# A 3x3 convolution on TensorE as 32x32 taps in place of 128x64 matmuls, in a Fourier tower of four layers

## The chip, the cores and the metric

One core of a Trainium2 chip. The metric is the device time of one execution in microseconds, the median of three runs. Everything is float32. TensorE is the matmul engine, VectorE, ScalarE and GpSimd (POOL) the others; SyncE (SP) issues most loads. PSUM is where matmuls put their results, in 8 banks of 512 columns.

## The reference

32 images of 64x64 pixels with 3 channels are lifted to 32 channels (`h = concat(grid, x) @ P_w + P_b`). Then four layers run, each of which is a spectral branch and a 3x3 convolution of the same input:

```python
for i in range(nl):
    h_ft = jnp.fft.rfft2(h)
    out_modes = jnp.einsum('bixy,ioxy->boxy', h_ft[:, :, :mx, :my], w_c)      # 16 x 16 modes
    spec = jnp.fft.irfft2(out_modes, s=(H, W))
    conv = lax.conv_general_dilated(h, conv_w[i], (1, 1), 'SAME', dimension_numbers=dn) + conv_b[i]
    h = leaky(spec + conv)
out = leaky(h @ Q1_w + Q1_b) @ Q2_w + Q2_b
```

The result, 32 x 64 x 64, goes through two small attention blocks (the tail, not touched by the change).

## The kernel before, in words

`build_tower` computes the four layers, `build_tail` the rest. The tower works on pairs of images: 16 pairs a layer, so T = 16 l + p runs from 0 to 63. A pixel has a row parity r and a column parity s; the 32 channels of the four parities (r, s) lie on 4 x 32 partitions. What a partition holds of a pair is 64 rows of 32 pixels. Output is made in four units u of 512 pixels each, each in its own PSUM bank (`acc[0]` to `acc[3]`).

On TensorE a pair T needs these groups:
- `convolve(T, u)` (L343 to L366). In layer 0 it is one 96x128 matmul from columns prepared on the host (L355). In layers 1 to 3 it reads `halo` (L365), which is unfolded in one direction: the four partition groups hold the four column phases that two output columns need, and each row parity has its own plane. Three row taps by two output row parities make 6 matmuls of 128x64 with 512 columns. The weights (`conv`) hold zeros where a phase isn't used by a column parity.
- `spectral(T, u)` (L368 to L377): the last step of the inverse transform, added to the same bank: 16 matmuls of 128x32 with 128 columns.
- `rows_forward(n)` (L272), `columns_forward(n)` (L285): forward transforms of the activations of pair n − 2; both are followed by other engines. `columns_back(T)` (L334): the first step of the inverse.
- `mix(l)` (L317): once a layer, the product over channels for all modes, 128 matmuls in four parts.
- in layer 3 `head_hidden` (L380) and `head_out` (L393) in place of the forward transforms.

A float32 matmul appears in the profile as two MATMUL and two LDWEIGHTS records.

The order on every engine is written by hand, and semaphores join them. TensorE's order of a pair is in `pair(l, p, last)` (L400): convolve 0 and 1, spectral 0 and 1, rows_forward, convolve 2 and 3, columns_forward, columns_back of the next pair, spectral 2 and 3. Between layers (L449 to L458) it is rows_forward, convolve 0, columns_forward, convolve 1, mix, convolve 2, columns_back, convolve 3. VectorE transposes (`turn_x` L573 from `x_now` to `xt`; `turn_rows` L580; `turn_modes` L596; `turn_back` L603). ScalarE evicts each unit with bias and leaky ReLU to `x_now` (`evict`, L506), and copies the spectrum (`spectrum`, L489) with 8 activations a pair. GpSimd stores `x_now` to DRAM (L246), and SP loads `halo` for pair T from there (L203), double buffered, when pair T − 2 has left it. `rows_forward`, `columns_back` and their transposes share the banks 4 and 5 (`turned`), `columns_forward` uses bank 6. `convolve(T, u)` waits only for the eviction of the same unit of the pair before (L346).

## Time and profile before

| | us |
|---|---|
| median of 3 runs (range) | 1410.2 (1409.04 to 1412.42) |
| the profiled execution | 1409.31 |
| its span, first to last instruction | 1407.5 |
| TensorE busy in the span | 1268.3 (90%) |
| VectorE busy | 546.8 (39%) |
| ScalarE busy | 492.0 (35%) |
| mean granted TensorE clock | 0.945 of 2.4 GHz |
| MATMUL records, LDWEIGHTS records | 17040, 17040 |

A MATMUL record lasts until its result is written, so records overlap, and busy time counts a stretch that holds at least one. In the timeline a row merges the records of one group: its start, the time from the first start to the last end, engine, line, operation, the operands with the shape of one record, the count, and in brackets the idle time before it and what ended that. The time for which a group holds the array is read from the start of the next one.

### The profile page before, as it was taken

What the parts mean: (1) busy time and instruction counts of PE and PEld (TensorE: products, weight loads), DVE (VectorE), ACT (ScalarE), POOL (GpSimd) and SP (SyncE); (2) the same over time, 40 slices, a digit from 0 to 9 for tenths busy, and PEclk for the clock granted to TensorE, in tenths of its full rate; (3) what the DMA queues carried; (4) which work ended last, traced back from release to release, by engine and by line L of the source; (5) the groups of instructions that cost most, each with busy time, mean ns of one, the idle gap of its engine ahead of it and who ended that gap; (6) DMA issues with size and microseconds to landing.
All of it is one profiled execution on the core that took longest, in us unless ns stands there. A gap on an engine that the chain in (4) does not pass through costs nothing. (4 is left out here: it accounts for less than half of the span.)

```text
span 1407.5 us, 36967 instructions
## 1 busy us (share of the span) xinstructions
PE 1268.3 (90%) x17040; PEld 694.0 (49%) x17040; DVE 546.8 (39%) x553; ACT 492.0 (35%) x934; POOL 66.7 (5%) x122
## 2 busy tenths in 40 slices
PE   4888889899999998999999989999999962889955
PEld 2555455544444444444444445444444422579945
DVE  3655555333335332433343332111111103567775
ACT  1244344233333332233333322443444431425511
POOL 2000000000000000000000000111111010000000
PEclk7899999999999999999999999999999976879967
DMA  8434344776666666766666664555555507000000
GB/s 273 156 119 117 112 128 126 248 205 186 186 186 188 189 191 178 239 189 189 188 193 197 180 193 103 123 119 117 116 115 117 115 4 153 2 1 1 2 0 15
DMA packets 39338, 192.19 MB, mean 137 GB/s; under 512 B 16432, under 2 KB 16560, under 8 KB 17456
## 3 DMA queue, kind: packets, MB, share of 16 engines
q1 hardware_dynamic: 30224, 137.39, 38.3%
q0 software_dynamic: 8960, 52.44, 10.3%
q8 instruction: 134, 2.20, 0.7%
q14 instruction: 20, 0.16, 0.0%
HBM read 136.84 MB, written 52.95 MB: 135 GB/s over the span
## 5 line engine op out<-in xcount | busy, mean ns | idle before, releaser
L365 PE MATMUL psum<-halo,conv 128*64 128x512 f32 x2304 | 521.1, 600 | 0.0
L365 PEld LDWEIGHTS psum<-halo,conv 128*64 128x64 f32 x2304 | 156.4, 137 | 326.7 <-issue 288.4
L603 DVE STREAM_TRANSPOSE vt<-psum 128x1024 f32<-128x1024 f32 x64 | 127.4, 1990 | 391.0 <-PE psum L341 391.0
L489 ACT ACTIVATE spec<-psum 32x128 f32<-32x128 f32 x384 | 150.5, 392 | 299.2 <-PE psum L294 295.3
L506 ACT ACTIVATE x_now<-psum,conv_bias 128x512 f32<-128x512 f32 x256 | 169.8, 687 | 243.7 <-PE psum L376 226.2
L376 PEld LDWEIGHTS psum<-dft,vt 128*32 128x32 f32 x8192 | 216.0, 110 | 76.9 <-issue 72.4
L376 PE MATMUL psum<-dft,vt 128*32 128x128 f32 x8192 | 250.2, 274 | 1.0 <-DVE vt L603 1.0
L573 DVE STREAM_TRANSPOSE xt<-x_now 128x1024 f32<-128x1024 f32 x100 | 124.1, 1243 | 283.3 <-PE psum L282 186.3
L580 DVE STREAM_TRANSPOSE ft<-psum 128x1024 f32<-128x1024 f32 x50 | 95.1, 1901 | 12.6 <-PE psum L282 12.6
L294 PEld LDWEIGHTS psum<-dft,ft 128*64 128x64 f32 x1600 | 55.1, 141 | 62.3 <-DVE ft L580 43.0
L294 PE MATMUL psum<-dft,ft 128*64 128x64 f32 x1600 | 57.5, 227 | 27.1 <-DVE ft L580 27.1
L341 PE MATMUL psum<-zt,dft 64*64 64x256 f32 x1024 | 71.8, 393 | 0.3 <-DVE zt L596 0.3
L513 ACT ACTIVATE xt<-psum,q1b 128x512 f32<-128x512 f32 x64 | 40.5, 684 | 87.8 <-PE psum L389 87.8
L521 ACT ACTIVATE ft<-psum,q2b 4x512 f32<-4x512 f32 x64 | 43.5, 680 | 77.1 <-PE psum L397 76.5
L282 PE MATMUL psum<-xt,dft 64*32 64x512 f32 x800 | 57.9, 638 | 12.9 <-DVE xt L573 12.9
L355 PE MATMUL psum<-xcol,conv 96*128 96x512 f32 x128 | 65.5, 634 | 0.0
L246 POOL DMA_DIRECT2D activations<-x_now x48 | 25.7, 535 | 804.5 <-ACT x_now L506 804.5
L773 PE MATMUL t_psum<-t_consts 128*128 128x128 f32 x212 | 28.2, 299 | 26.3 <-DMA t_consts<-in_tail 26.3
L341 PEld LDWEIGHTS psum<-zt,dft 64*64 64x64 f32 x1024 | 35.7, 133 | 25.8 <-issue 15.6
L253 POOL DMA_DIRECT2D tower_out<-ft x64 | 31.6, 501 | 287.6 <-ACT ft L521 287.5
L773 PEld LDWEIGHTS t_psum<-t_consts 128*128 128x128 f32 x212 | 27.6, 215 | 29.7 <-DMA t_consts<-in_tail 28.1
L950 ACT ACTIVATE t_prob<-t_dif 128x512 f32<-128x512 f32 x32 | 20.2, 631 | 59.6 <-DVE t_dif L1065 59.6
(133 smaller groups left out, 785.4 us busy)
## 6 DMA issues: line engine op xcount, KB each, us to landing
activations<-x_now POOLq DMA_DIRECT2D x48, 1056.0 KB, 10.1
halo<-activations SPq DMA_DIRECT2D x192, 264.0 KB, 6.5
halo<-activations SPq DMA_DIRECT2D x192, 263.9 KB, 6.2
wspec<-in_spec SPq DMA_DIRECT2D x16, 1024.0 KB, 9.5
xcol<-in_xcol SPq DMA_DIRECT2D x16, 384.0 KB, 4.4
x_now<-in_ser SPq DMA_DIRECT2D x2, 1056.0 KB, 6.6
t_lq<-in_onehot SPq DMA_DIRECT2D x1, 2048.0 KB, 15.3
t_kr<-in_causal SPq DMA_DIRECT2D x1, 2048.0 KB, 23.9
```

The costliest lines, as they stand in the source:

```text
L282: z = mm(turned[g:g + 32, r, :], ex[64 * r:64 * r + 64, :], xt[64 * r:64 * r + 64, 32 * h + m:32 * h + 32:2, :], start=True, stop=True)
L294: z = mm(ap_[64 * h:64 * h + 64, 64 * kyb:64 * kyb + 64], ft[:, k0:k0 + 2, :].rearrange("p a c -> p (a c)"), ey[:, ri, :], start=(ri == 0) ...
L341: z = mm(turned[64 * il:64 * il + 64, cg, 256 * ri:256 * ri + 256], iy[64 * cg:64 * cg + 64, m, :], zt[64 * cg:64 * cg + 64, :, 2 * p:2 * ...
L355: mm(acc[u], conv0[:], xcol[:, k, HALF * u:HALF * u + HALF], start=True, stop=False, skip_group_check=True)
L365: mm(acc[u][64 * r:64 * r + 64, :], conv[:, l - 1, dy, :], rows[:, at:at + 16, 0:G], start=(dy == 0), stop=False, skip_group_check=True)
L376: z = mm(acc[u][g:g + 32, 128 * ih:128 * ih + 128], vt[:, k, 4 * u + ih, r, :], ix[:, s, :], start=False, stop=True, skip_group_check=True)
L489: z = copy(spec[g:g + 32, 64 * qh:64 * qh + 64, ql, 2 * p:2 * p + 2] .rearrange("p (y x) b -> p y b x", x=MODES), ap_[32 * q:32 * q + 32]. ...
L506: copy(x_now[:, k, 16 * u:16 * u + 16, 0:G], acc[u].rearrange("p (i j) -> p i j", j=G), ACT.Prelu, bias=conv_bias[:, l:l + 1], alpha=SLOPE ...
L573: vec.transpose(xt[:, 32 * h:32 * h + 32, :], x_now[:, n % 2, 32 * h:32 * h + 32, 0:G]).then_inc(s_xt, 1)
L580: vec.transpose(ft[:].rearrange("p k c -> p c k"), turned.rearrange("p a b -> p (a b)").rearrange("p (i c) -> p c i", c=C)).then_inc(s_ft, 1)
L603: vec.transpose(vt[:, k].rearrange("p h r o -> p (h r) o").rearrange("p y o -> p o y"), turned.rearrange("p a b -> p (a b)").rearrange("p ...
L773: mm(bank(b)[:, 0:128], ident, ident, start=True, stop=True)
```

## The change

The convolution of layers 1 to 3 is written as nine taps of 32 channels by 32 channels. `halo` now holds every pixel once: the four parities f on 4 x 32 partitions, one plane, with zero rows around. For a tap, input parity f feeds output parity f ^ d, where d says which of row and column parity differ: d = 3 has 4 taps (both differ), d = 1 and d = 2 have 2, d = 0 has 1. For each tap, 16 matmuls of 32x32 with 512 columns are issued, one for each input parity f and output position `to`; the unit is u = f ^ d ^ to. So that the four units of one tap fall on different positions, the output parities of unit u are permuted by u (`turn`), and the other matmuls and the halo's loads of layers 2 and 3 (16 DMAs of 16 rows in place of 8) undo it. All four units are started together, and the convolution of a pair is cut into four segments, `taps(T, 3)`, `(T, 1)`, `(T, 2)`, `(T, 0)`; each waits for the last matmul of the segment before (`s_seg`). `rows_forward`, `columns_forward` and `columns_back` are cut into twice as many, smaller matmuls. The banks are shared otherwise: `rowed` (4, 5), `backed` (6, 7), `columned` (4). The orders of TensorE, ScalarE and VectorE are changed. `head_out` writes all 128 partitions, and `head_read` is one activation. In the cut diff below the removed lines of the old `convolve`, `pair` and the order between layers are left out (they stand above), as are the layout of weights on the host and the constants.

```diff
-PAD = 2 * PITCH
-HALO = 2 * PLANE + PAD
+UNIT = 16 * PITCH
+TOP = 1 + 2 * PITCH
+HALO = TOP + PLANE + 2 * PITCH + 1
...
-        turned = psum[:, 4:6, :]
-        ap_ = psum[:, 6, 0:256]
+        rowed = psum[:, 4:6, :]
+        backed = psum[:, 6:8, :]
+        hidden = psum[:, 4:6, :]
+        valued = psum[:, 4, :]
         spare = psum[:, 7, :]
+
+        def columned(n):
+
+            return psum[:, 6 if n < 2 else 4, 0:256]
...
+        def turn(l, u):
+
+            return u if l > 0 else 0
...
+                if src >= 2:
+                    sp.wait_ge(s_acc, 4 * (T - 2) + 4)
+                if l == 1:
+                    sp.dma_start(halo[:, k, TOP:TOP + PLANE], x_d[p]).then_inc(s_halo[k], 16)
+                    return
+                for u in range(4):
+                    for f in range(4):
+                        g = 32 * (f ^ turn(l - 1, u))
+                        sp.dma_start(halo[32 * f:32 * f + 32, k, TOP + UNIT * u:TOP + UNIT * u + UNIT],
+                                     x_d[p, g:g + 32, UNIT * u:UNIT * u + UNIT]).then_inc(s_halo[k], 16)
...
+                if n > 2:
+                    pe.wait_ge(s_spec, n)
+                l = (n - 2) // PAIRS if n >= 2 else 0
+                for i in range(2):
+                    for m in range(2):
+                        for h in range(2):
+                            for f in range(2):
+                                u, g = 2 * h + i, 64 * m + 32 * h
+                                at = 16 * u + m
+                                z = mm(rowed[g:g + 32, f ^ (turn(l, u) // 2), 256 * i:256 * i + 256],
+                                       ex[64 * f:64 * f + 64, turn(l, u) % 2, :],
+                                       xt[64 * f:64 * f + 64, at:at + 15:2, :], start=True, stop=True)
                 z.then_inc(s_fx, 1)
...
-                            k0 = ri * MODES + 4 * kyb + 2 * h
-                            z = mm(ap_[64 * h:64 * h + 64, 64 * kyb:64 * kyb + 64],
-                                   ft[:, k0:k0 + 2, :].rearrange("p a c -> p (a c)"), ey[:, ri, :],
-                                   start=(ri == 0), stop=(ri == 1))
+                            for i in range(2):
+                                k0, g = ri * MODES + 4 * kyb + 2 * h + i, 64 * h + 32 * i
+                                z = mm(columned(n)[g:g + 32, 64 * kyb:64 * kyb + 64], ft[:, k0, :], ey[:, ri, :],
+                                       start=(ri == 0), stop=(ri == 1))
                 z.then_inc(s_fy, 1)
...
+                reached(pe, s_vt, T)
                 for m in range(4):
                     il, ri = m // 2, m % 2
-                    for cg in range(2):
-                        z = mm(turned[64 * il:64 * il + 64, cg, 256 * ri:256 * ri + 256],
-                               iy[64 * cg:64 * cg + 64, m, :],
-                               zt[64 * cg:64 * cg + 64, :, 2 * p:2 * p + 2, :].rearrange("p k b o -> p k (b o)"),
-                               start=True, stop=True)
+                    for h in range(2):
+                        for cg in range(2):
+                            g = 64 * il + 32 * h
+                            z = mm(backed[g:g + 32, cg, 256 * ri:256 * ri + 256],
+                                   iy[64 * cg:64 * cg + 64, m, 32 * h:32 * h + 32],
+                                   zt[64 * cg:64 * cg + 64, :, 2 * p:2 * p + 2, :].rearrange("p k b o -> p k (b o)"),
+                                   start=True, stop=True)
                 z.then_inc(s_v, 1)
...
+            def convolve_first(T):
+
+                k, p = T % 2, T % PAIRS
+                pe.wait_ge(s_xcol[k], 16 * (p // 2 + 2))
+                for u in range(4):
+                    reached(pe, s_x, 4 * (T - 1) + u + 1)
+                    mm(acc[u], conv0[:], xcol[:, k, HALF * u:HALF * u + HALF], start=True, stop=False,
+                       skip_group_check=True)
+
...
+            def taps(T, d):
 
                 l, p = place(T)
                 k = T % 2
+                if d == 3:
+                    pe.wait_ge(s_x, 4 * T)
+                    pe.wait_ge(s_halo[k], halo_loads(T))
+                else:
+                    pe.wait_ge(s_seg, 3 * (T - PAIRS) + {1: 1, 2: 2, 0: 3}[d])
+                for dy in ((-1, 1) if d & 2 else (0,)):
+                    for dx in ((-1, 1) if d & 1 else (0,)):
+                        w = 3 * (dy + 1) + dx + 1
+                        for f in range(4):
+                            r, s = (f ^ d) // 2, (f ^ d) % 2
+                            di, dj = (r + dy - f // 2) // 2, (s + dx - f % 2) // 2
+                            for to in range(4):
+                                u = f ^ d ^ to
+                                at = TOP + (16 * u + 2 * di) * PITCH + dj
+                                rows = halo[32 * f:32 * f + 32, k, at:at + UNIT].rearrange("p (i j) -> p i j", j=PITCH)
+                                z = mm(acc[u][32 * to:32 * to + 32, :], conv[32 * f:32 * f + 32, l - 1, w, :],
+                                       rows[:, :, 0:G], start=(d == 3 and dy == -1 and dx == -1), stop=False,
+                                       skip_group_check=True)
+                if d > 0:
+                    z.then_inc(s_seg, 1)
+                elif p > 0:
+                    z.then_inc(s_acc, 2)
 
...
-                            g = 64 * r + 32 * s
+                            g = 32 * ((2 * r + s) ^ turn(l, u))
                             z = mm(acc[u][g:g + 32, 128 * ih:128 * ih + 128], vt[:, k, 4 * u + ih, r, :],
                                    ix[:, s, :], start=False, stop=True, skip_group_check=True)
-                z.then_inc(s_acc, 1)
+                if u >= 2 or l == 0 or p == 0:
+                    z.then_inc(s_acc, 1)
...
+            def first_pair(p):
+                T = p
+                if p > 0:
+                    convolve_first(T)
+                    rows_forward(T + 1)
+                    if p < LAST:
+                        columns_back(T + 1)
+                for u in range(4):
+                    spectral(T, u)
+                if p > 0:
+                    columns_forward(T + 1)
+                else:
+                    columns_back(T + 1)
+            def pair(l, p):
 
                 T = l * PAIRS + p
+                if p == 0:
+                    for u in range(4):
+                        spectral(T, u)
+                    columns_back(T + 1)
+                    return
+                taps(T, 3)
+                rows_forward(T + 1)
+                if p < LAST:
+                    columns_back(T + 1)
+                taps(T, 1)
+                spectral(T, 0)
+                taps(T, 2)
+                spectral(T, 1)
+                taps(T, 0)
+                spectral(T, 2)
+                spectral(T, 3)
+                columns_forward(T + 1)
+            def last_pair(p):
+                T = (NL - 1) * PAIRS + p
+                if p == 0:
+                    for u in range(4):
+                        spectral(T, u)
+                    columns_back(T + 1)
+                    return
+                taps(T, 3)
+                head_hidden(p - 1, 0)
+                taps(T, 1)
+                head_hidden(p - 1, 2)
+                taps(T, 2)
+                head_out(p - 1)
                 spectral(T, 0)
                 spectral(T, 1)
+                taps(T, 0)
+                spectral(T, 2)
+                spectral(T, 3)
                 if p < LAST:
                     columns_back(T + 1)
+            def boundary(l):
+                T = l * PAIRS
+                taps(T, 3)
+                rows_forward(T + 1)
+                taps(T, 1)
+                columns_forward(T + 1)
+                pe.wait_ge(s_spec, T + 2)
+                mix(l)
+                columns_back(T)
+                taps(T, 2)
+                taps(T, 0)
 
...
-                copy(hid[:, u, :], psum[:, 6 + u % 2, :], ACT.Prelu, bias=q1b[:], alpha=SLOPE).then_inc(s_hid, 1)
+                copy(hid[:, u, :], hidden[:, u % 2, :], ACT.Prelu, bias=q1b[:], alpha=SLOPE).then_inc(s_hid, 1)
...
-                for u in range(4):
-                    z = copy(h_now[32 * u:32 * u + 4, k, :], psum[32 * u:32 * u + 4, 6, :], ACT.Identity,
-                             bias=q2b[32 * u:32 * u + 4, :])
-                z.then_inc(s_h, 1)
+                copy(h_now[:, k, :], valued, ACT.Identity, bias=q2b[:]).then_inc(s_h, 1)
 
...
                 if last and p > 0:
-                    head_activate(p - 1, 0)
-                    head_activate(p - 1, 1)
-                evict(T, 0)
-                evict(T, 1)
-                if p > 0:
-                    if last:
-                        head_activate(p - 1, 2)
-                        head_activate(p - 1, 3)
-                        head_read(p - 1)
-                    else:
-                        spectrum(T - 1)
-                evict(T, 2)
-                evict(T, 3)
+                    for u in range(4):
+                        head_activate(p - 1, u)
+                    head_read(p - 1)
+                for u in range(4):
+                    evict(T, u)
+                if p > 0 and not last:
+                    spectrum(T - 1)
                 if p == LAST and not last:
                     spectrum(T)
             for u in range(4):
...
-                    if not last:
-                        turn_x(T + 2, 0)
-                        if p > 0:
-                            turn_rows(T + 1)
+                    if p > 0 and not last:
+                        turn_rows(T + 1)
                     if p < LAST:
                         turn_back(T + 1)
                     if not last:
+                        turn_x(T + 2, 0)
```

The three calls `convolve(0, 0..3)` around `project` and `mix(0)` become one `convolve_first(0)` after `columns_back(0)`. The order of layer 0 is `first_pair`, that of layers 1 and 2 `pair`, of layer 3 `last_pair`, and `boundary(l)` runs ahead of each layer but the first.

## Rows read from the trace of the kernel before

**Rows 1.** Stretches, layer 1: us; busy of PE, PEld, DVE, ACT, POOL; clock; DMA share, GB/s.
```profile
282.00:542.00 260.00, 260.00 (x3612) 126.73 (x3604) 99.55 (x64) 85.54 (x177) 7.97 (x15) 1.00 0.66 191
```

**Rows 2.** Timeline of TensorE, layer 1, one pair and the starts around it.
```profile
600.29 1.09 PE L282 MATMUL psum<-xt,dft 64*32 64x512 f32 x16
601.31 5.37 PE L365 MATMUL psum<-halo,conv 128*64 128x512 f32 x24
606.51 1.10 PE L294 MATMUL psum<-dft,ft 128*64 128x64 f32 x32
607.54 1.11 PE L341 MATMUL psum<-zt,dft 64*64 64x256 f32 x16
608.58 1.96 PE L376 MATMUL psum<-dft,vt 128*32 128x128 f32 x64
610.46 5.37 PE L365 MATMUL psum<-halo,conv 128*64 128x512 f32 x24
615.76 1.95 PE L376 MATMUL psum<-dft,vt 128*32 128x128 f32 x64
617.65 1.09 PE L282 MATMUL psum<-xt,dft 64*32 64x512 f32 x16
```

**Rows 3.** Timeline of TensorE, layer 0, one pair.
```profile
218.65 1.09 PE L282 MATMUL psum<-xt,dft 64*32 64x512 f32 x16
...
222.99 1.15 PE L294 MATMUL psum<-dft,ft 128*64 128x64 f32 x32 [1.34 <-DVE ft L580]
...
230.79 1.09 PE L282 MATMUL psum<-xt,dft 64*32 64x512 f32 x16
```

**Rows 4.** Timeline of TensorE, layer 3, one pair.
```profile
1056.83 1.09 PE L389 MATMUL psum<-x_now,q1w 32*32 32x512 f32 x16
1057.85 1.96 PE L376 MATMUL psum<-dft,vt 128*32 128x128 f32 x64
...
1075.25 1.09 PE L389 MATMUL psum<-x_now,q1w 32*32 32x512 f32 x16
```

**Rows 5.** Line L797 in the tail: durations min/median/max, starts, form.
```profile
L797 PE MATMUL t_psum<-t_zT,t_uT x64: 218/218/267, 1190.1 to 1191.1; 64*64 64x64 f32 x64
```

**Rows 6.** Timeline of ScalarE in the pair of rows 2.
```profile
600.42 0.69 ACT L506 ACTIVATE x_now<-psum,conv_bias 128x512 f32<-128x512 f32 x1 [0.18 <-PE psum L376]
607.66 3.24 ACT L489 ACTIVATE spec<-psum 32x128 f32<-32x128 f32 x8 [6.54 <-PE psum L294]
610.92 1.27 ACT L506 ACTIVATE x_now<-psum,conv_bias 128x512 f32<-128x512 f32 x2
```

**Rows 7.** Line L203, the halo's loads: issue, landing; and the queue of instructions.
```profile
L203 SPq DMA_DIRECT2D halo<-activations x384: 302/422/2221, 239.3 to 1110.8; - x192
...
DMA to landing us min/median/max: 3.0/6.5/11.5
...
q8 instruction: 134, 2.20, 0.7%
```

**Rows 8.** Timeline of TensorE and VectorE between layers 0 and 1.
```profile
248.36 1.95 PE L376 MATMUL psum<-dft,vt 128*32 128x128 f32 x64
...
255.29 4.45 PE L365 MATMUL psum<-halo,conv 128*64 128x512 f32 x12
...
263.90 7.69 PE L329 MATMUL psum<-spec,wspec 128*64 128x64 f32 x256 [0.66 <-ACT spec L489]
...
277.86 1.95 PE L376 MATMUL psum<-dft,vt 128*32 128x128 f32 x64
...
271.63 1.25 DVE L596 STREAM_TRANSPOSE zt<-psum 128x1024 f32<-128x1024 f32 x1 [0.62 <-PE psum L329]
```

**Rows 9.** Timeline after mix(0), and ScalarE at the tower's end.
```profile
54.96 1.12 PE L355 MATMUL psum<-xcol,conv 96*128 96x512 f32 x2
...
59.54 1.96 PE L376 MATMUL psum<-dft,vt 128*32 128x128 f32 x64 [1.00 <-DVE vt L603]
...
1140.83 2.75 ACT L521 ACTIVATE ft<-psum,q2b 4x512 f32<-4x512 f32 x4 [4.97 <-PE psum L397]
```

More of the change, by code:

```diff
@@ L1300, in tower_inputs @@
     spec[:, :, 1, ..., 0, :], spec[:, :, 1, ..., 1, :] = wi, wr
+    values = np.zeros((4, C, 2, C), np.float32)
+    for g in range(4):
+        for e in range(2):
+            values[g, :, e, g ^ (2 * e)] = np.asarray(t["L0_tok_Q2_w"])[:, 0]
     four = lambda b: np.tile(np.asarray(b).reshape(-1), 4).reshape(128, 1)
```

139 lines of the change are left out of this document (35 added, 104 removed).

## The prediction

> **What bounds the kernel now.** I first read the table of stretches: in layer 1 TensorE is busy for all of a stretch of 260 us, at the full granted clock (1.00, the 2.4 GHz level), while VectorE and ScalarE are busy 38% and 33% of it [rows 1]. So only TensorE's list of groups matters there, and I read its timeline by starts, since the next group's start is where the array was given over. One image pair of layers 1 and 2 takes 617.65 − 600.29 = 17.36 us [rows 2]: convolve of two units 5.20, columns_forward 1.03, columns_back 1.04, spectral of two units 1.88, convolve 5.30, spectral 1.89, rows_forward 1.01. Layer 0 takes 12.14 us a pair, of it 1.34 us of waiting for VectorE's transpose before columns_forward [rows 3]. Layer 3 takes 18.42 [rows 4].
>
> **What a group costs.** A float32 matmul shows as two records. In convolve a record has 512 columns and two run side by side (64 output columns each): 24 records in 5.16 us plus a change of group is 0.43 us per record and tile. The same 0.43 explains rows_forward (16 records on 8 tiles of 64x32: 0.86, measured 1.02) and head_hidden (16 records on 8 tiles of 32x32: 0.86, measured 1.02) [rows 2, 4]. So the price is rounds x 0.43 us plus about 0.15 us for a change of tile shape. Over one pair: 10.32 (convolve) + 3 x 0.86 (rows, columns, back) + 3.49 (spectral: 128 records on 4 tiles at 0.109 us a round) = 16.39; the other 0.97 us is six changes of shape, 0.16 each.
>
> **The convolution.** 24 matmuls of 128x64 become 144 of 32x32 a pair (segments 3, 1, 2, 0 have 64, 32, 32, 16), so 48 records become 288. Before, a quarter of the weights fed were zeros (each output parity uses three of the four column phases); now only the nonzero taps run. If 16 tiles run side by side the price is 288/16 = 18 rounds x 0.43 = 7.74 us against 10.32. The trace shows no 16 tiles at once. The bound below is that, 7.74. The bound above is the most tiles that it does show, 8 [rows 4]: 288/8 x 0.43 = 15.5 us. Which is nearer? What could cap it is start spacing, weight loads or outputs. Start spacing: on 64x64 tiles with 64 columns, 64 records start within 1.0 us (1190.1 to 1191.1), 16 ns a record [rows 5], and the taps need 27 ns (7.74 us / 288), the pace at which spectral already runs (1.88 us for 64 [rows 2]). Loads: spectral also loads 32 columns for each record at that pace. Different data to four column tiles of one row group is what spectral does. What is unproved is four row groups times four column groups, and four banks written for each 32 partitions; two are shown (rows_forward). I take 16 tiles.
>
> One rule speaks against the change. In each round one bank takes output of four row groups, at four different quarters of the partitions. In head_hidden four row groups write one bank at different quarters too, and two units of it take 1.02 us, the 8-tile price [rows 4]. The Trainium skill, page TensorEngine Tiling (Array Packing), section Gotcha 1: PSUM Pressure, says that different row tiles cannot access the same bank at the same time. By that rule head_hidden would have taken 8 rounds of 2, 3.4 us; the trace does not agree, and I price nothing for it. For 16 tiles only a page has a price: the Trainium skill, page TensorE: Matmul & The Clock Gate, section Measured speedup vs the span model, gives one duration plus 4 ns for each further tile; the taps would then cost what I take, and no row here shows it.
>
> **The new pair, layers 1 and 2**, in order of the code: four tap segments 7.74, plus for each a change of shape and a start staggered over 16 tiles, 0.21 (estimate, from 0.16 with 8 tiles): 8.58. rows_forward 1.02. columns_back is now 32 records on 8 tiles of the same shape as rows_forward: 0.96. spectral 0 and spectral 1 alone: 0.87 + 0.14 = 1.01 each. spectral 2 and 3: 1.88. columns_forward, now 64 records of 64 columns on 4 tiles: at 16 ns a record [rows 5], no change of shape: 1.0. Sum 15.46, a gain of 1.90. 15 pairs in each of two layers: **57 us**.
>
> **Its waits.** taps(T, 3) starts all four units, so it waits for the eviction of unit 3 of the pair before; behind it all of TensorE is queued. An eviction starts 0.13 us after the group behind its spectral starts and takes 0.69 us [rows 6], two back to back 1.27. Units 0 and 1 are released after taps(T, 0), so from the start of spectral 2: evictions start at 0.2, 0.8, 1.4 and 2.0 and the last ends at 2.7, while columns_forward ends at 1.88 + 1.0 = 2.9. Hidden, with 0.2 us to spare. rows_forward now waits for ScalarE's spectrum (it shares bank 4 with it): 3.24 us from 0.12 us after columns_forward [rows 6], ending at 3.4, against 3.65 for the first tap segment. Hidden, 0.25 to spare. If either cover fails by 0.3 us, 45 pairs cost 13 us: for the range. The wait of taps on its own last segment is covered by the group between, except once a layer (0.16 us).
> Halo loads: half the bytes, 1 DMA a pair in layer 1 and 16 in layers 2 and 3 in place of 8. SP needs 16 x 0.42 = 6.8 us to issue them and the landing is 6.5 [rows 7]: 13.3 us after the release, and 16.4 are there (columns_forward and one pair). Priced at nothing; with the longest landing, 11.5, 2 us late. Queued behind them on SP is only the next pair's load, on POOL nothing changes.
>
> **Layer 0.** convolve_first of four units together 3.63, rows_forward 1.02, columns_back 0.96, spectral 3.63, columns_forward 1.03: 10.3 against 12.14, since VectorE's 1.9 us transpose now lies behind columns_back and spectral. 15 pairs x 1.84 = **28 us**.
>
> **Layer 3.** taps, head_hidden, taps, head_hidden, taps are all of one tile shape: 3.44 + 0.86 + 1.72 + 0.86 + 1.72 + 0.6 of starts = 9.2; head_out 0.98, spectral 1.88, taps 1.07, spectral 1.88, columns_back 1.04: 16.05 against 18.42. ScalarE's two activations of hid (1.27) lie behind 1.8 us of taps. 15 x 2.37 = **35 us**.
>
> **Boundaries, start and end.** From the last spectral of a layer (248.36 + 1.88) to the first of the next (277.86) it is 27.6 us [rows 8]; there are three such boundaries. The 3.95 us wait for xt goes: the first tap segment lies in front of it. What is late next: mix now waits 3.4 us for spectrum with nothing in front of it, and columns_back 1.5 us for the last transpose of mix (1.25 us, from 0.21 after mix). Sum: 3.65 + 1.02 + 1.93 + 0.22 + 1.03 + 3.4 + 7.5 + 1.5 + 1.03 + 1.93 + 0.16 + 1.07 = 24.5. At 255.29 the first 12 records of convolve took 4.28 in place of 2.7 us after such an idle stretch, so the 3.4 us may cost up to 1.7 in mix: gain 1.4 to 3.1 a boundary, I take the middle, **7 us** for three. Start: 54.96 to 59.54 is 4.58 us, and it becomes 1.4 + 1.03 + 3.63 = 6.1, as all of convolve_first lies behind columns_back: **−1.5** [rows 9]. End: head_read is one activation of 0.69 in place of four, 2.75 us, twice on the path (before the evictions at 1143.6 and at the very end): **+4** [rows 9].
>
> **Sum.** 57 + 28 + 35 + 7 − 1.5 + 4 = 129.5 us. The profiled execution took 1409.3 us (span 1407.5), 0.9 below the median shown, 1410.2. 1410.2 − 129.5 = 1280.7, and I say 1280.
>
> **Rivals.**
> *Hand-offs or instructions bind, not the array.* A pair has 2 x 544 PE instructions in place of 2 x 240. The queue of instructions moved 2.20 MB in 134 pieces [rows 7], 64 bytes for each of the 34080 matmul and load instructions; the fastest long stretch of the trace, mix, takes 512 of them in 7.5 us (7.69 with the end of the last) [rows 8]. If that were the most that can be fed, a pair would take 1088/512 x 7.5 = 15.9 us, 0.5 more: with the thin covers above failing too, 0.5 to 1 us in 45 pairs, 1300 to 1325. Against it: 16 ns a record in [rows 5], though for 1 us only.
> *The array holds only 8 of these tiles at once.* Place: every tap segment. Then 15.5 us of taps, a pair of 23.2 us: 45 x 7.74 = 348 more than forecast, 1628. It decides from below about 13 tiles at once, where 288 x 0.43 / n exceeds the 9.6 us at which a pair is even. For it: nothing in the trace is wider than 8. Against it: nothing in the starts of head_hidden, 8 tiles within one 0.43 us round, looks like a limit.
>
> **How the numbers follow.** Forecast and its close variants (1262 to 1295) 0.72; fed or handed over late (1295 to 1340) 0.16; tiles capped, slower 0.10; the rest 0.02. The low end, 1262, is 0.1 us less for each start of a tap segment (45 x 4 x 0.1 = 18 us); the high end, 1330, takes in most of the second case. A measurement of this kernel tells 0.2% (3 us) from no change; forecast and second case are faster, the third slower.
>
> **What would show it.** In the profile after: a tap record every 27 ns, 18 rounds of 0.43 in a pair; starts of rows_forward 15.5 us apart in layers 1 and 2, 10.3 in layer 0, 16.0 in layer 3; no idle of TensorE before taps (ScalarE's eviction) or before rows_forward (spectrum); a 3.4 us idle before mix. Wrong if the taps' busy time over 45 pairs is far from 8.6 us a pair, or if idle time of TensorE put down to ScalarE or to issue passes 10 us in the tower.

## The result: slower, 1429.7 us against 1409.7

The changed kernel took 1429.71 us, median of 4 runs (1425.49 to 1434.98), against 1409.65 for the kernel before in the same session (4 runs, 1409.04 to 1412.42): ratio 1.014, 95% interval 1.0096 to 1.0185. The prediction was 1280 (1262 to 1330). Of all executions reported here one, 1412.62 us of e1_wide, is over 1.5% above the fastest of its kernel at a lower granted clock (0.931), and its ratio leaves it out. The profiled execution took 1425.49 us, span 1423.7, the fastest of the four; the 16.2 us over the profiled execution of before is what has to be explained, and the 145.7 us by which the forecast (1409.3 − 129.5 = 1279.8) fell short of it.

### Where the time went, by layer

From here a layer's span is the time from the last `spectral` record of its pair 0 to that of its pair 15, and a boundary the time from there to the last one of the next layer's pair 0, both read from the trace:

| us | layer 0 | layer 1 | layer 2 | layer 3 | three boundaries |
|---|---|---|---|---|---|
| before | 185.9 | 259.3 | 259.3 | 275.1 | 98.4 |
| after | 162.1 | 300.5 | 274.3 | 258.7 | 103.4 |
| pair before | 12.14 | 17.36 | 17.36 | 18.42 | |
| pair after | 10.25 to 11.9 | 17.7 to 24.1 | 16.9 to 20.9 | 17.25 | |

Sum: −23.8 + 41.2 + 15.0 − 16.4 + 5.0 = +21.0; outside the tower's pairs 4.8 came back. So two layers gained, two lost, and in the two that lost the pairs differ by 4 and 6 us. Before, nearly all pairs of a layer were alike. The written order is the same for each of them, which points to something from outside it.

The page of after: busy by engine, queues (packets, MB, share), and the costliest groups.

```profile
PE 1258.6 (88%) x31984; PEld 798.9 (56%) x31984; DVE 546.4 (38%) x553; ACT 453.6 (32%) x886; POOL 67.0 (5%) x121
...
q8 instruction: 251, 4.11, 1.2%
...
L399 PE MATMUL psum<-halo,conv 32*32 32x512 f32 x13824 | 536.1, 603 | 12.9 <-issue 12.7
...
L399 PEld LDWEIGHTS psum<-halo,conv 32*32 32x32 f32 x13824 | 217.1, 103 | 201.8 <-issue 140.3
```

TensorE is busy 9.7 us less than before, yet the kernel is slower: idle time has come in, and its releaser is "issue", no engine and no data. The queue of instructions moves 251 pieces in place of 134 [rows 7]. Layer 1, the stretch of [rows 1], is now:

```profile
282.00:542.00 260.00, 236.85 (x6983) 127.11 (x6967) 84.70 (x55) 71.09 (x154) 6.46 (x13) 0.96 0.34 111
```

TensorE was busy for all 260.00 us of it before, and is for 236.85. The clock column has fallen too, from 1.00 to 0.96. In the trace's record of the clock this is 20.5 us in layer 1 at the 1.2 GHz level, in four stretches (from 291.9, 387.4, 466.0 and 506.9 us). The first follows 0.9 us after an idle of TensorE of 1.04 us, the others begin within idles of 1.45, 2.39 and 3.56 us. In layer 1 of before there is no such stretch, and none in layers 2 and 3 of either kernel. The timeline of TensorE in after, in order of time: a pair of layer 0 [rows 3], the first boundary [rows 8], a gap in layer 1, one undisturbed pair of layer 2 [rows 2], a pair of layer 3 [rows 4].

```profile
80.23 1.09 PE L302 MATMUL psum<-xt,dft 64*32 64x256 f32 x32
...
90.48 0.88 PE L302 MATMUL psum<-xt,dft 64*32 64x256 f32 x24
...
239.56 9.23 PE L350 MATMUL psum<-spec,wspec 128*64 128x64 f32 x256 [3.20 <-ACT spec L563]
250.15 1.13 PE L365 MATMUL psum<-zt,dft 64*32 64x256 f32 x32 [1.35 <-DVE zt L661]
...
257.33 2.38 PE L416 MATMUL psum<-dft,vt 128*32 128x128 f32 x76 [0.91 <-issue]
...
308.40 1.08 PE L399 MATMUL psum<-halo,conv 32*32 32x512 f32 x14
310.85 2.23 PE L399 MATMUL psum<-halo,conv 32*32 32x512 f32 x50 [1.37 <-issue]
...
622.44 1.09 PE L302 MATMUL psum<-xt,dft 64*32 64x256 f32 x32
623.32 1.27 PE L365 MATMUL psum<-zt,dft 64*32 64x256 f32 x32
624.53 2.35 PE L399 MATMUL psum<-halo,conv 32*32 32x512 f32 x64
626.81 1.08 PE L416 MATMUL psum<-dft,vt 128*32 128x128 f32 x32
627.82 2.35 PE L399 MATMUL psum<-halo,conv 32*32 32x512 f32 x64
630.10 1.08 PE L416 MATMUL psum<-dft,vt 128*32 128x128 f32 x32
631.11 1.16 PE L399 MATMUL psum<-halo,conv 32*32 32x512 f32 x32
632.19 1.96 PE L416 MATMUL psum<-dft,vt 128*32 128x128 f32 x64
633.97 1.08 PE L316 MATMUL psum<-dft,ft 128*32 128x64 f32 x64
634.97 4.46 PE L399 MATMUL psum<-halo,conv 32*32 32x512 f32 x128
639.37 0.88 PE L302 MATMUL psum<-xt,dft 64*32 64x256 f32 x24
...
1054.14 1.07 PE L439 MATMUL psum<-xt,q2w 128*32 128x512 f32 x8
...
1071.38 1.07 PE L439 MATMUL psum<-xt,q2w 128*32 128x512 f32 x8
```

The undisturbed pair, by starts: 639.37 − 622.44 = 16.93 us, where 15.46 was forecast. The four tap segments hold the array for 4.40, 2.28, 2.28 and 1.08 us: 10.04, where 8.58 was forecast; all else together takes 6.89, and 6.88 was forecast. And most pairs of layer 1 aren't undisturbed: between 308.40 and 310.85 TensorE has put 14 of the segment's 64 records out and waits for nothing that the profile shows.

### Two theories

**A, the feed.** A pair is 1088 PE instructions in 17 us. Instructions come in pieces of 16 KB, 256 instructions, one per 4 us at this rate. In the trace's list of packets pieces start at 298.34, 301.65, then only at 308.41, and again at 311.99. Between 301.65 and 308.41 the pair's halo load (issued at 301.10) and the store of the pair before it (issued at 302.04) hold the same DMA engines:

```profile
301.10 0.32 SPq L215 DMA_DIRECT2D halo<-activations  x1
302.04 0.53 POOL L261 DMA_DIRECT2D activations<-x_now  x1 [19.98 <-ACT x_now L580]
```

Each landed 6 to 8 us after it was issued, and the gap of TensorE follows. It ends at 310.85, 2.43 us after the start of the late piece. The same holds through the whole layer: from 262.5 to 560 us TensorE has 16 gaps over 0.2 us, and each of them ends 2.2 to 2.6 us after the start of a piece that itself came 5.5 to 8.6 us after the one before it, where the median is 4.0. Layer 3 has halo loads but no store, 57 PE instructions per us in place of 64, and no gap. The waits of TensorE around layer 1, from 260 to 560 us (total, times, longest; short ones aren't listed):

```profile
PE psum L399 <- issue: 12.2, 9, 3.6
PE psum L302 <- issue: 8.1, 4, 2.8
PE psum L365 <- issue: 5.9, 3, 2.4
```

**B, the array.** Even undisturbed, the taps take 17% more than was forecast for 16 tiles at 0.43 us a round. The starts of matmuls in the segment at 607.02 (first records, from the trace): 16 from 607.022 to 607.122, one each 7 ns; the 17th at 607.905, as soon as the first tile is free; but the 18th only at 608.098, and then one each 16.7 ns. The first matmul's second record ended at 607.475 + 0.587 = 608.06 (starts are measured, the ends of TensorE's records are modelled). It stays so in the four-tap segment at 634.97: the 18th starts 0.036 us after the end of the first, and each of the 39th to the 48th 0.035 to 0.037 us after the end of the one 17 before it. So either TensorE holds no more than 17 float32 matmuls (68 instructions: two loads, two passes each) that haven't completed (window, W), or 16 tiles at once stream more slowly for a reason in the array or its output (R).

A rival to both: **C**, DMA traffic slows matmuls themselves, not their feed.

### The profile page after: what moved, and what is told of

Same layout as the page of the kernel before. It is cut to its first block and busy times, and to the rows that moved or that the text cites. A ratio compares the mean times of both kernels' runs of the same rounds, so it can differ in the third digit from the quotient of the medians.

```text
span 1423.7 us, 67011 instructions
## 1 busy us (share of the span) xinstructions
PE 1258.6 (88%) x31984; PEld 798.9 (56%) x31984; DVE 546.4 (38%) x553; ACT 453.6 (32%) x886; POOL 67.0 (5%) x121
## 5 line engine op out<-in xcount | busy, mean ns | idle before, releaser
L399 PE MATMUL psum<-halo,conv 32*32 32x512 f32 x13824 | 536.1, 603 | 12.9 <-issue 12.7
L399 PEld LDWEIGHTS psum<-halo,conv 32*32 32x32 f32 x13824 | 217.1, 103 | 201.8 <-issue 140.3
L416 PEld LDWEIGHTS psum<-dft,vt 128*32 128x32 f32 x8192 | 218.6, 110 | 113.6 <-issue 105.0
L416 PE MATMUL psum<-dft,vt 128*32 128x128 f32 x8192 | 256.2, 275 | 3.6 <-issue 3.5
L365 PE MATMUL psum<-zt,dft 64*32 64x256 f32 x2048 | 85.8, 384 | 17.2 <-issue 11.8
L302 PE MATMUL psum<-xt,dft 64*32 64x256 f32 x1600 | 62.1, 397 | 15.5 <-issue 14.3
L365 PEld LDWEIGHTS psum<-zt,dft 64*32 64x32 f32 x2048 | 47.2, 107 | 37.3 <-issue 18.0
L316 PE MATMUL psum<-dft,ft 128*32 128x64 f32 x3200 | 56.9, 221 | 8.3 <-issue 4.2
L302 PEld LDWEIGHTS psum<-xt,dft 64*32 64x32 f32 x1600 | 26.0, 109 | 66.8 <-issue 58.8
L316 PEld LDWEIGHTS psum<-dft,ft 128*32 128x32 f32 x3200 | 52.4, 111 | 13.7 <-DVE ft L645 7.4
L431 PE MATMUL psum<-x_now,q1w 32*32 32x512 f32 x512 | 54.8, 593 | 2.2 <-ACT xt L587 1.4
L350 PE MATMUL psum<-spec,wspec 128*64 128x64 f32 x1024 | 35.3, 239 | 11.6 <-ACT spec L563 9.6
```

The source lines that it names most:

```text
L302: z = mm(rowed[g:g + 32, f ^ (turn(l, u) // 2), 256 * i:256 * i + 256], ex[64 * f:64 * f + 64, turn(l, u) % 2, :], xt[64 * f:64 * f + 64, ...
L316: z = mm(columned(n)[g:g + 32, 64 * kyb:64 * kyb + 64], ft[:, k0, :], ey[:, ri, :], start=(ri == 0), stop=(ri == 1))
L365: z = mm(backed[g:g + 32, cg, 256 * ri:256 * ri + 256], iy[64 * cg:64 * cg + 64, m, 32 * h:32 * h + 32], zt[64 * cg:64 * cg + 64, :, 2 * p ...
L399: z = mm(acc[u][32 * to:32 * to + 32, :], conv[32 * f:32 * f + 32, l - 1, w, :], rows[:, :, 0:G], start=(d == 3 and dy == -1 and dx == -1) ...
L416: z = mm(acc[u][g:g + 32, 128 * ih:128 * ih + 128], vt[:, k, 4 * u + ih, r, :], ix[:, s, :], start=False, stop=True, skip_group_check=True)
L431: z = mm(hidden[to:to + 32, u % 2, :], q1w[32 * g:32 * g + 32, :], x_now[32 * g:32 * g + 32, p % 2, 16 * u:16 * u + 16, 0:G], start=True, ...
```

## The experiments

Ratios with an interval come from 4 or more runs of each kernel; the others are one execution.

### e1_wide: fewer instructions, the same taps

```diff
-                            for i in range(2):
-                                k0, g = ri * MODES + 4 * kyb + 2 * h + i, 64 * h + 32 * i
-                                z = mm(columned(n)[g:g + 32, 64 * kyb:64 * kyb + 64], ft[:, k0, :], ey[:, ri, :],
+                            k0 = ri * MODES + 4 * kyb + 2 * h
+                            z = mm(columned(n)[64 * h:64 * h + 64, 64 * kyb:64 * kyb + 64],
+                                   ft[:, k0:k0 + 2, :].rearrange("p a c -> p (a c)"), ey[:, ri, :],
...
```

(and `columns_back` in its old 64-wide form.)

> The changed kernel with columns_forward and columns_back as wide as before (16 and 8 matmuls a pair in place of 32 and 16), so 992 in place of 1088 TensorE instructions a pair; nothing else differs. Theory A (in layers 1 and 2 TensorE starves for instructions, whose 16 KB pieces queue behind the burst of halo load and store at the end of each pair): fewer instructions to feed, so the mean pair falls from 20.0 us (layer 1) and 18.3 us (layer 2) by 0.3 to 1 us, 10 to 30 us in all, 1400 to 1420. Rival B (the idle time is a wait for the halo or the spectrum, shown as issue): no gain, perhaps 0.1 us a pair lost by two more changes of tile shape, 1430 to 1440.

Measured 1388.8 us (1383.35 to 1412.62), ratio 0.983 [0.978, 0.988]: 41 us less than after, beyond the 10 to 30 expected. A clean pair takes 17.09 us, 0.16 longer than in after; the spans of layers 1 and 2 fell to 286.6 and 257.2, that of layer 3 stayed (258.5). Instructions that cost the array nothing cost the kernel time where data moves. That is A, with a steeper price than I gave it.

### e2_twelve: three of four output positions

```diff
-                            for to in range(4):
+                            for to in range(4 if d == 3 and w == 0 else 3):
```

(The outputs of position 3 lack eight of their nine taps, so the convolution is incomplete.)

> The changed kernel in which the taps leave out the output position 3 (12 of 16 tiles, 108 + 4 of 144 matmuls a pair), except in the first tap of segment 3. Theory W (TensorE holds about 64 instructions, that is 16 float32 matmuls, until they complete, so a matmul of a tile starts only when the one 16 before it is complete: 1.07 us a tap in place of 0.86): with 12 tiles the window reaches a third of a tap ahead, the two taps of segment 1 take 1.9 to 2.0 us in place of 2.28, and segment 3 about 3.8 in place of 4.40. Rival R (16 streams contend for SBUF or PSUM, cost in proportion to the tiles): each tap still takes over 1.0 us, 2.1 to 2.2 for two, and starts within a tap are not spaced at 7 ns.

```profile
587.92 2.21 PE L399 MATMUL psum<-halo,conv 32*32 32x512 f32 x48
590.07 1.08 PE L416 MATMUL psum<-dft,vt 128*32 128x128 f32 x32
```

Two taps took 2.15 us (2.28 with 16 tiles), one execution 1352.7. By size alone this is R's 2.1 to 2.2, and W's 1.9 to 2.0 missed. The starts decide, and against R, which had said that they are not 7 ns apart: 12 from 587.924, one each 7 ns; then 13 to 17 from 588.809, one each 7 ns as their tiles come free; and the 18th at 589.000, though its tile was free. The first matmul's second record ended at 588.376 + 0.588 = 588.964. With 12 tiles as with 16 it is the 18th that waits, for completion of the first. My 1.9 to 2.0 for W had left out that the first five are taken at the tile's pace and the rest at 16.7 ns.

### e9_eight: eight tiles at a time

```diff
-                            for to in range(4):
+                                for to in (2 * half, 2 * half + 1):
```

(with `for half in range(2)` around the taps of a segment.)

> The changed kernel in which each tap segment runs its taps first on the output positions 0 and 1 and then on 2 and 3, so that 8 of 16 tiles are at work at a time; the same 144 matmuls a pair. Theory W (a matmul waits for the completion of the one 17 before it): with 8 tiles the 17th matmul is two rounds later, 1.75 us, and the first is complete by then, so the window never bites: every round takes 0.43 us, segments of two taps 3.6 to 3.7 us, four taps 7.1, one tap 1.9, together 16.3 us a pair of convolution, a pair 23.2, and at 47 instructions a us there are no gaps: about 1620 to 1640. Rival (a stall of 0.2 us at every 17th matmul, whatever is in flight): 0.4 us more in a segment of two taps, 0.8 in one of four, the pair 25.

```profile
631.55 3.08 PE L400 MATMUL psum<-halo,conv 32*32 32x512 f32 x64
634.55 1.08 PE L417 MATMUL psum<-dft,vt 128*32 128x128 f32 x32
```

1518.4 us; a clean pair 20.43 us, where W had 23.2 and 1620 to 1640 in all: both missed. Two taps take 3.00 us: not the 3.44 of 8 rounds, because the second half, on tiles that are idle, starts inside the first half's last rounds. Here the tiles of the second half had been idle from the start, yet only its first matmul begins early (at 0.64 us, as no. 17 of the program), and no. 18 at 1.08, just after the first of all completes (0.454 + 0.587 = 1.04). Why no. 17 doesn't start sooner stays open. So the 16 tiles do run side by side in after: its taps take 10.04 us a pair, and some 13.5 here. The rival of "8 tiles at once" is out, since what 8 at a time costs is measured, and after does not show it. The third part of W's expectation, no gaps, missed too: layer 1 took 317.5 us, 11 more than 15 clean pairs, with idle time put down to issue.

### e10_onepass: two instructions a matmul in place of four

```diff
-                                z = mm(acc[u][32 * to:32 * to + 32, :], conv[32 * f:32 * f + 32, l - 1, w, :],
-                                       rows[:, :, 0:G], start=(d == 3 and dy == -1 and dx == -1), stop=False,
+                                z = mm(acc[u][32 * to:32 * to + 32, :],
+                                       conv[32 * f:32 * f + 32, l - 1, w, :].bitcast(BF16)[:, 1::2],
+                                       rows[:, :, 0:G].bitcast(BF16)[:, :, 1::2], start=(d == 3 and dy == -1 and dx == -1), stop=False,
```

> The changed kernel in which the taps read only the upper two bytes of each number in the halo and in the weights, as bf16: the convolution is less exact, and a matmul is one load and one pass in place of two of each. It asks what the window counts. If it holds 64 to 68 instructions, 32 to 34 such matmuls, two whole taps, are in flight: 0.213 us a tap, the four taps of segment 3 in 1.0 to 1.1 us. If it holds 17 matmuls of any kind, a tap takes about 0.41 us and segment 3 1.4 to 1.5 us. Either way few gaps, since 288 instructions a pair are gone.

```profile
608.97 0.69 PE L400 MATMUL psum<-halo,conv 32*32 32x512 bf16 x32
609.59 1.08 PE L418 MATMUL psum<-dft,vt 128*32 128x128 f32 x32
...
617.80 1.10 PE L303 MATMUL psum<-xt,dft 64*32 64x256 f32 x32 [1.16 <-ACT spec L565]
...
622.01 0.68 PE L400 MATMUL psum<-halo,conv 32*32 32x512 bf16 x29 [1.72 <-issue]
```

Two taps, 32 matmuls, take 0.62 us, with no stall before the 18th: the second 16 start 0.25 us after the first, while the first matmul still runs (its record lasts 0.41 us). Were the limit 17 matmuls of any kind, or the outputs of 16 tiles, it would be here too. Here 17 matmuls are 34 instructions and not 68. That fits a limit on instructions; one on weight loads or on passes alone, of which a float32 matmul has two each, would look the same. So B is W, and what exactly its window counts is shown only so far. The run, 1201.35 us, also shows what is next: its pairs in layer 1 take 13.1 to 18.3 us, in layer 3 12.06, with idle time put down to issue and, for the first time, to ScalarE's spectrum.

### e3_paced: the halo load in four parts

```diff
...
                 for u in range(4):
+                    reached(sp, s_seg, 3 * (T - 1 - PAIRS) + min(u + 1, 3) if T > PAIRS else 0)
+                    if l == 1:
+                        sp.dma_start(halo[:, k, TOP + UNIT * u:TOP + UNIT * u + UNIT],
+                                     x_d[p, :, UNIT * u:UNIT * u + UNIT]).then_inc(s_halo[k], 16)
+                        continue
...
```

(The old load for l = 1 and the new count that TensorE waits for aren't shown.)

> The changed kernel with the halo load of pair T cut into four units, each issued only after a tap segment of pair T - 1, so that loads no longer run together with the store and no megabyte of loads stands ahead of an instruction piece. Theory A: the gaps of 1.5 to 2.3 us once a pair in layer 1 go or halve, layer 1 falls from 20.0 to 17.5 to 18.5 us a pair, layer 2 from 18.3 to 17.3 to 18, together 30 to 55 us: 1375 to 1400. Rival C (the rate of instructions alone is too high for the feed, 64 a us, whatever the data do): within 10 us of 1430.

1427.1 us (1419.86 to 1436.39), ratio 1.0138 [1.0076, 1.02]: no gain, a miss. Layer 1 did what A says (271.5 in place of 300.5), but in layer 2 the load is now itself late, since its last 8 DMAs are issued only after the third segment:

```profile
590.30 2.73 PE L401 MATMUL psum<-halo,conv 32*32 32x512 f32 x33 [2.96 <-DMA halo<-activations]
```

Layer 2 took 296.6: from 560 to 870 us TensorE waits 28.2 us for the halo, and 4.3 us of idle time are put down to issue, 12.7 in after. A burst was traded for a wait on data.

### e4_quiet: the same instructions, no traffic

```diff
+                if T >= PAIRS + 2:
+                    return
                 sp.wait_ge(s_store[src % 2], 16 * (src // 2 + 1))
...
-            for X in range((NL - 1) * PAIRS):
+            for X in range(PAIRS):
```

(The kernel leaves out the loads that bring the pixels of later pairs, so its convolution reads old ones.)

> The changed kernel with halo loads only for the first two pairs of layer 1 and no stores after layer 0; the later pairs convolve what lies in the halo, so almost no data move by DMA in layers 1 to 3. Every TensorE instruction stays. Theory A: no gaps, 16.9 to 17.1 us for each pair of layers 1 and 2 (17.0 is what the fastest pairs of the changed kernel take), about 1425 - 75 = 1350. Rival C (instruction rate alone): pairs stay at 18 to 20 us, over 1400.

```profile
607.15 1.09 PE L303 MATMUL psum<-xt,dft 64*32 64x256 f32 x32
...
624.08 1.09 PE L303 MATMUL psum<-xt,dft 64*32 64x256 f32 x32
```

1356.05 us. Pairs take 16.93 us nearly everywhere, spans 256.4 and 258.2 in layers 1 and 2; layer 0, whose traffic is kept, is as in after. All 251 pieces are fetched. The granted clock of layers 1 and 2 is 1.00. So traffic is what makes the gaps. It tells A from "1088 instructions a pair are too many by themselves", but not from C. For that I read two tap segments of after by stretches, a two-tap one and the four-tap one at 634.97 (the last two columns are the DMA engines' share and GB/s):

```profile
624.53:626.81 2.28, 2.28 (x68) 0.81 (x65) 2.28 (x2) 0.00 (x0) 0.00 (x0) 1.00 0.65 150
...
634.97:639.37 4.40, 4.40 (x136) 2.13 (x129) 1.22 (x2) 3.11 (x8) 0.53 (x1) 1.00 0.84 308
```

In the midst of 308 GB/s the four taps last 4.40 us, as here (619.69 to 624.08) with next to none. Traffic does not slow matmuls that TensorE has; C is out. The run also shows what the change is worth with hardly a gap: 1409.3 − 1356.1 = 53 us, not 130.

### e5_storelate: the store after the load, not beside it

```diff
                 pool.wait_ge(s_x, 4 * X + 4)
+                if X >= PAIRS:
+                    pool.wait_ge(s_seg, 3 * (X + 1 - PAIRS) + 2)
```

> The changed kernel with the store of pair X, in layers 1 and 2, issued only after the second tap segment of the next pair, some 8 us later, so that it no longer runs right behind the halo load. Theory A (an instruction piece waits behind load and store together): the gap after each pair shortens from about 2 us to below 1, layer 1 from 20.0 to about 18.5 us a pair, layer 2 from 18.3 to 17.5: 1385 to 1410. Rival D (each burst of a megabyte by itself is enough to delay a piece, so two bursts at two places cost as much as one long one): 1420 to 1440.

1382.28 us (1381.13 to 1388.43), ratio 0.982 [0.980, 0.984]; layer 1 at 269.8, layer 2 at 265.6, a little better than the 1385 to 1410 expected. No part of these layers ran at the lower clock. The same bytes and the same instructions, 47 us less than after. This is the cleanest run for A: only when a transfer starts was changed.

### e6_order: the kernel before with the new order alone

```diff
+            def first_pair(p):
+
+                T = p
+                if p > 0:
+                    for u in range(4):
+                        convolve(T, u)
+                    rows_forward(T + 1)
+                    if p < LAST:
+                        columns_back(T + 1)
+                for u in range(4):
+                    spectral(T, u)
```

(with the banks `rowed`, `backed`, `columned`, and ScalarE's and VectorE's order in layer 0; the convolution is the old one.)

> The kernel before, with its convolution of 128x64 matmuls and its halo, and of the change only the order and the banks: first_pair for layer 0, evictions ahead of the spectrum there and at a layer's last pair, separate banks for rows_forward, columns_back and columns_forward, and convolve ahead of rows_forward between layers. By the sum of the prediction for these parts: layer 0 12.14 to 10.4 us a pair (26 us), the three boundaries 3 to 4 us each, the start 1.5 lost: 1410 - 34 = 1376, 1370 to 1385. Rival: if the gain of layer 0 came from the smaller matmuls and not from the order, layer 0 stays at about 12 us a pair and the kernel at 1400 or above.

1377.44 us (1375.77 to 1378.51), ratio 0.978 [0.976, 0.979]. Layer 0 took 155.8 (pairs 10.4), layers 1 to 3 were as before (17.36, 18.42). The last two boundaries fell from 33.7 and 32.3 to 29.6 and 30.1; the first rose from 32.4 to 36.2, with TensorE waiting 4.21 us for the halo before its convolution. So 32 us of what the change offered had nothing to do with taps, and the rest of the change, the taps with the smaller matmuls and the order around them, lost 1429.7 − 1377.4 = 52 us on top.

### e7_shapes: the taps in three shapes, 80 matmuls in place of 144

```diff
...
+                if d == 4:
+                    for o in range(4):
+                        for u in range(4):
+                            z = one(u, o ^ u, 0, 128, 9 + o, 0, 0)
+                elif d == 2:
+                    for s in range(2):
+                        for r in range(2):
+                            for u in range(4):
+                                o = 2 * r + s
+                                z = one(u, o ^ u, 64 * (1 - r), 64, 13 + s, -1 if r == 0 else 1, 0)
...
```

(Taps that read the same pixel offset from all four parities are one matmul of 128 rows, those from two parities one of 64 rows, the other three of 32; with e1's `columns_forward`.)

> The changed kernel with the nine taps in three tile shapes: four taps that read the same offset as one 128x32 matmul, two as one 64x32, three as 32x32: 80 matmuls a pair in place of 144, the same 9 rounds of the array; columns_forward as wide as before. Theory W (16 to 17 float32 matmuls at most are in flight): the 128x32 and 64x32 rounds run at 0.86 us, only the three 32x32 rounds at 1.07: convolution 8.4 us in place of 10.05, a clean pair 15.4 to 15.7 us in place of 16.93. Theory A: 768 in place of 1088 instructions a pair, so few gaps: 1409 - 26 (layer 0) - 50 (layers 1, 2) - 35 (layer 3) = 1290 to 1320. Rival R (contention of many streams): the 64x32 segment too takes over 2.1 us and the pair stays above 16.3.

```profile
599.95 3.64 PE L393 MATMUL psum<-halo,conv 128*32 128x512 f32 x32
603.52 1.09 PE L302 MATMUL psum<-xt,dft 64*32 64x256 f32 x32
604.41 1.24 PE L365 MATMUL psum<-zt,dft 64*32 64x256 f32 x30
...
607.33 1.08 PE L435 MATMUL psum<-dft,vt 128*32 128x128 f32 x32
608.34 2.35 PE L393 MATMUL psum<-halo,conv 32*32 32x512 f32 x64
610.62 1.08 PE L435 MATMUL psum<-dft,vt 128*32 128x128 f32 x32
611.63 1.16 PE L393 MATMUL psum<-halo,conv 32*32 32x512 f32 x32
...
619.26 1.09 PE L302 MATMUL psum<-xt,dft 64*32 64x256 f32 x32
```

**1292.18 us (1289.79 to 1292.73), ratio 0.917 [0.915, 0.918]: the fastest of all kernels with the whole float32 convolution.** Only nonzero weights run, as in after, but four tiles of 128 rows at a time fill the array with 4 matmuls. The four-tap segment takes 3.57 us (4.40 in after): 8 rounds of 0.43 and a start. The two-tap segment of 64x32 tiles takes 2.05 us (605.28 to 607.33) and starts while columns_back's last records run, that of 32x32 tiles 2.28. A pair takes 15.74 us, under the 16.3 that R asked for and 0.04 above W's range; the convolution takes 9.0 us, where W had 8.4. And with 768 PE instructions a pair the feed keeps up; of TensorE's long waits in layer 1 put down to issue this is left:

```profile
PE psum L393 <- issue: 0.2, 1, 0.2
```

### e8_shapes_late: both cures together

```diff
                 pool.wait_ge(s_x, 4 * X + 4)
+                if X >= PAIRS:
+                    pool.wait_ge(s_seg, 3 * (X + 1 - PAIRS) + 2)
```

(on e7_shapes.)

> e7_shapes with the store of layers 1 and 2 issued after the second tap segment of the next pair. If the store right behind the halo load still costs gaps in e7_shapes, this is 5 to 20 us faster than it; if there are none left, within 3 us of it.

1296.22 us (1296.11 to 1305.51), ratio 0.922 [0.919, 0.925]: no better than e7, rather 4 us worse, for which no run gives a cause; layers 1 and 2 take 239.7 and 235.9 us, in e7 238.8 and 235.9. Where the feed keeps up, moving the store buys nothing. What was worth 47 us on one kernel is worth nothing on the other, and that is what A asks for.

## Why the prediction was wrong

**The step that failed first** is "If 16 tiles run side by side the price is 288/16 = 18 rounds x 0.43 = 7.74 us". They do run side by side, but a new matmul also waits until the one 17 places ahead has completed, and for most of them that is later than their tile being free (1.08 us after its start, by the 18th, against 0.88, by the 17th). A tap costs 1.1 us, not 0.86. Over a pair 10.04 against 8.58 (with starts): 1.47 us, in 30 pairs 44 us. With the 1.2 us by which layer 3's 17.25 exceeds the forecast 16.05 (15 pairs, 18 us) this is 62 of the 146 us missed. I had bounded the price by the number of tiles, 8 or 16, and had "start spacing, weight loads or outputs" as what could cap it. How many matmuls may be unfinished was not on the list, since in before no group has more than 8 tiles at work.

**The second** is the price of the rival "Hand-offs or instructions bind": "0.5 more", "0.5 to 1 us in 45 pairs". The rival was right that instructions can come too late, and wrong in how. It set a highest mean rate, and there is no such limit in reach here: the undisturbed pairs are fed 1088 instructions in 16.93 us, and e4 feeds nearly all pairs so. What the runs show is single pieces that come late behind a burst of data, up to 8.6 us after the one before where 4.0 is the median. I had taken the rate from mix, in a stretch where the DMA engines were idle. The prediction's own sign of this, over 10 us of idle time put down to issue, came out at 42 us on four lines of the page alone (L302, L399, L365, L416). Against pairs of 16.93 us it cost 300.5 − 254 = 46.5 us in layer 1, 274.3 − 254 = 20.3 in layer 2, none in layer 3; in layer 0, against the forecast's 10.3, 7.6. Together 74 of the 146. Not all of it is waiting: in the 20.5 us of layer 1 at 1.2 GHz TensorE worked for 19, and at full clock would have needed half of that, so about 9.5 of the 46.5 us (an estimate) are the clock that fell after gaps. The prediction had priced a fallen clock only at the boundaries.

**Boundaries** were to give 7 us and cost 5.0: 12 more. The two idles came as forecast, 3.20 before mix (3.4) and 1.35 before columns_back (1.5), and mix ran after the first at a granted clock that averaged 0.67 of the full one for 3.5 us, so 9.23 us in place of 7.69 [rows 8]. I had priced that at up to 1.7. What was not in the sum are again the gaps of the feed, 0.91 and more. The start and end gained 4.8 where 2.5 was forecast. Sum: 44 + 18 + 74 + 12 − 2 = 146.

**What held.** Eviction and spectrum are covered: inside the pairs of layers 1 and 2 TensorE waits for neither. ScalarE in the pair of the timeline:

```profile
614.93 2.48 ACT L580 ACTIVATE x_now<-psum,conv_bias 128x512 f32<-128x512 f32 x4 [18.36 <-PE psum L399]
617.61 3.19 ACT L563 ACTIVATE spec<-psum 32x128 f32<-32x128 f32 x8 [0.21 <-PE psum L316]
```

The evictions end at 617.41, 0.05 us before the next pair's taps start at 617.46 (I had said 0.2 to spare); the spectrum ends at 620.80, 1.6 before rows_forward. The halo was never late, layer 0's clean pair is 10.25 as forecast, and different row groups writing one bank cost nothing that the starts show: 16 tiles in four banks start 7 ns apart.

**The rivals.** "8 tiles at once" would give 1518 (e9), not 1628. The slower side of my forecast held 0.10 and named the wrong mechanism; what made the kernel slower than before was the window and the late instructions, each of them less than the gain, adding up to more: 62 and 74 against 129.5.

**What stays open.** Why pieces of instructions wait behind data: whether the engine that fetches them takes its queues in turn, or how many pieces TensorE holds ahead, no run tells. Nor does one tell why starts are 16.7 ns apart, and not 7, once the window binds. e3's order with fewer, larger DMAs wasn't tried, nor 32x32 taps with fewer weight loads.

## What to carry to other kernels

Cutting a matmul into more and smaller ones keeps the array full only as far as the count of unfinished instructions allows: here a float32 matmul is four, so 17 are in the air, and rounds of 16 tiles lose the time from "tile free" to "complete". Fill the array with the tallest tiles that hold no zeros, and count the PE instructions per us beside the rounds; at 64 per us a burst of DMA at the wrong moment stops TensorE, at 53 (e9) it still does so for less, at 49 (e7) hardly ever. A stop can cost more than itself, as the granted clock may fall behind it. If pairs that should be alike have uneven lengths, and idle time is put down to issue, look at when the pieces of the instruction queue start and what transfers lie between them.

## What the runs showed of the hardware

- Starts on 16 free tiles come one each 7 ns (after, at 607.02), and one each 16.7 ns once the limit binds. The 18th float32 matmul waits for completion of the first with 16, 12 and 8 tiles; with two instructions a matmul, 32 of them start without a stall. The Trainium skill, page Advanced Engine Details and Errata, section Engine Queue Depths, gives TensorE a queue of 64 entries, "complicated with tiling". The 17 x 4 = 68 instructions measured here, some of them in execution, come near it. That a float32 matmul counts until it has completed is what these runs add.
- A piece of 16 KB of instructions can come up to 4.6 us late (8.6 us after the one before, median 4.0) behind a load and a store of 1 MB each, and TensorE then stands for up to 3.6 us. The Trainium skill, page Runtime: NRT & Kernel Launch, section Instruction fetch mechanics, says that the fetch is hidden since the sequencer dispatches more slowly than instructions are refilled. In layer 3 of after, at 57 instructions per us and without a store, no idle time speaks against it; in layer 1, at 64 and with the traffic, the fetch is not hidden, and the measurement decides.
- TensorE's granted clock fell from the 2.4 to the 1.2 GHz level four times in layer 1 of after, after idles of 1.04 to 3.56 us, and not after others, one of 2.85 us among them.
